# Cluster sums of two units in three from bf16 parts, and the order of work around them

## The chip, the cores and the metric

One core of a Trainium2 chip runs the kernel. The metric is the time of one execution on the device in microseconds, the median over runs. The five engines (TensorE or PE, VectorE or DVE, ScalarE or ACT, GpSimd or POOL, SyncE or SP) each work through a queue of their own in program order and wait for each other by semaphores.

## What is computed

x is 8 batches of 512 channels by 1536 tokens (32 x 48), there are 40 centroids, and W is 512 x 512; all fp32.

```
xn = x / norm(x);  cn = centroids / norm(centroids)
idx = argmax over n of einsum('bchw,nc->bnhw', xn, cn)
onehot = one_hot(idx, N)
sum_x = einsum('bhwn,bchw->bnc', onehot, x)
centroids_local = sum_x / maximum(count, 1.0)
delta = centroids_local[idx] - x
alpha = exp(-mean(delta * delta, over channels))
y = x + alpha * delta
out = relu(einsum('oc,bchw->bohw', W, y) + b)
```

## The kernel before

A batch is cut into PARTS = 3 units of 512 tokens; there are 24 units, g = 3 b + u. For each unit, in the order of the data:

- `similarities` (L728): fp32 matmuls of x with the centroids, in two column tiles of 64 (one for each half of the tokens); `transpose_sims` turns them, and DVE finds the best cluster (`best_sims`, `first_best`, L324 to L339), which gives the one-hots `oh` (fp32). ScalarE makes `oh3` of them, three bf16 copies side by side (`copy_onehot`, L573); `transpose_onehot` (L752) and `evacuate_onehot` (L580) give `ohT`.
- DVE's `transpose_half` (L316) turns x, loaded a second time in blocks of 32 channels (`xs`), into `XT`, token by channel, in two halves a unit. `sum_clusters` (L768) multiplies `oh` and `XT` into the bank `sumP`: per unit two pairs of fp32 matmuls of 512 columns, one of each pair into partitions 0 to 63, the other into 64 to 127. One fp32 matmul of the program is two instructions in the trace.
- `copy_sums`, `low_clusters`, `add_halves`, `scale_means`, `high_means`, `rest_of_mean` and `parts_of_mean` make the means `G` in three bf16 parts.
- `gather` (L799) brings each token its mean (bf16 matmuls), half of the channels at a time; DVE's `delta` (L373) subtracts x; ScalarE's `square` (L531) and DVE's `add_squares`, `fold` and `low_sum` (L391), with ScalarE's `move_upper` and `high_sum` (L540) between, give the sum of squares in a high and a low part; `sum_squares` (L806) adds over partitions, `exp` (L544) makes alpha.
- DVE's `scale` (L397) multiplies by alpha, GpSimd's `y_half` (L286) adds x, ScalarE's `high_half` (L549) rounds y to its high part, GpSimd's `low_half` (L293) takes the low part. In the last units half of these is on DVE (L405, L412).
- `convolve` (L824 to L826): for each of four quarters o of the output channels, 12 matmuls (high x high, low x high, high x low) into one of two banks of `main`; ScalarE's `relu` (L557) empties it. A quarter may start when the quarter two before it is emptied.

The order is written out by hand, for each engine, in a loop over g from 3 to 23. Iteration g gathers unit g, convolves unit g - 2, and scales unit g - 1; p = g mod 3. The work for batch b + 1 stands beside it: with p = 0 and p = 1 (called first and second iteration here) its similarities, with p = 1 its one-hots on DVE, with p = 2 (third iteration) its cluster sums, means and the transposes of the next unit 0. The transposes of unit g + 4 stand in iteration g. GpSimd has a loop of its own over all units: two y halves, two low halves. SP's queue stores, then loads x when y has been made from what it overwrites, then loads `xs`.

The lines that set the places:

```
for g in range(PARTS, UNITS):          # PE
    gather(g, 0)
    if beside and p == 2:
        for u in range(PARTS):
            sum_clusters(b + 1, u)
        gather(g, 1)
        transpose_onehot(b + 1)
        convolve(g - LAG, 0)
        add_halves(b + 1)
```

Of the kernel before, what the change touches and what calls it, by code (L numbers as in the profile page):

```python
# [33 lines left out]

TAIL = UNITS - 1 - PARTS

DIRECT = 2


# [18 lines left out]
    return by_vector, 2 * g + h + 1 - by_vector  # L58


def folded(g):

    return max(0, g + 1 - DIRECT)


def build(nc, x, cent, w, bias, out):
# [3 lines left out]
    with ctx:  # L70
        def sb(name, shape, dt):
            return ctx.enter_context(nc.sbuf_tensor(name, shape, dt))
# [7 lines left out]
        X = [sb(f"x{j}", [P, KC, HW], F32) for j in range(2)]  # L80
        XS = [sb(f"xs{j}", [P, C // BLK, QT], F32) for j in range(2)]
        XT = sb("xt", [P, PARTS, TILES, C], F32)
        Z = [sb(f"z{j}", [P, KC, UNIT], F32) for j in range(2)]
        SQ = sb("sq", [P, 2, UNIT], F32)
        upper_sum = sb("upper_sum", [LOW, UNIT], F32)
# [66 lines left out]
        rc_step, mean_step, rest_step, g_ready = sem("rc_step"), sem("mean_step"), sem("rest_step"), sem("g_ready")  # L152
        gat_done, z_done, sq_done = sem("gat_done"), sem("z_done"), sem("sq_done")
        pair_done, s_done, sh_done, sl_done = sem("pair_done"), sem("s_done"), sem("sh_done"), sem("sl_done")
        upper_done, fold_done = sem("upper_done"), sem("fold_done")
        one_done, exp_done, za_done = sem("one_done"), sem("exp_done"), sem("za_done")
        y_pool, y_dve, hi_done = sem("y_pool"), sem("y_dve"), sem("hi_done")
# [21 lines left out]
        def squares(g, h):  # L179
            if g < DIRECT:  # L180
                return OUT[g][:, pair(h), :]
            return SQ[:, :, :] if h == 0 else gat[:, :, :]

        def plain(b):

# [72 lines left out]
        @block.gpsimd  # L258
        def _(pool):
            pool.memset(ident[:, :], 0.0).then_inc(ident_done, 1)  # L260
            pool.memset(ones[:, :].bitcast(F32), 1.0).then_inc(const_done, 1)
            pool.memset(select0, 0.0).then_inc(ident_done, 1)
            pool.memset(below2[:, :], 0.0).then_inc(ident_done, 1)
            pool.memset(below3[:, :], 0.0).then_inc(ident_done, 1)
            pool.wait_ge(ident_done, 4)
            pool.affine_select(out=ident[:, :], in_=ident[:, :], compare_op=ALU.not_equal, fill=1.0,
                               base=0, pattern=[[-1, P]], channel_multiplier=1).then_inc(ident_done, 1)
            pool.affine_select(out=select_rows, in_=select_rows, compare_op=ALU.not_equal, fill=1.0,
                               base=0, pattern=[[0, COPIES], [-1, N]], channel_multiplier=1).then_inc(ident_done, 1)
            for m, rows in ((below2, N), (below3, 2 * N)):  # L270
                pool.affine_select(out=m[:, :], in_=m[:, :], compare_op=ALU.is_gt, fill=-1.0,
                                   base=rows, pattern=[[0, 1]], channel_multiplier=-1).then_inc(const_done, 1)
            pool.wait_ge(ident_done, 6)
            pool.affine_select(out=select_rows, in_=select_rows, compare_op=ALU.not_equal, fill=1.0,
                               base=-NPAD, pattern=[[0, COPIES], [-1, N]], channel_multiplier=1
                               ).then_inc(ident_done, 1)
            pool.tensor_copy(identb[:, :], ident[:, :]).then_inc(const_done, 1)
            pool.wait_ge(ident_done, 7)
            pool.tensor_copy(select[:, :], select0).then_inc(const_done, 1)

            def y_half(g, h):
                if y_on_vector(g, h):
                    return
                pool.wait_ge(za_done, 2 * g + h + 1)
                z = Z[g % 2][:, pair(h), :]
                pool.tensor_tensor(z, z, X[g // PARTS % 2][:, pair(h), span(g)], ALU.add).then_inc(y_pool, 1)  # L286

            def low_half(g, h):
                if low_on_vector(g, h):
                    return  # L290
                pool.wait_ge(hi_done, 2 * g + h + 1)
                wait(pool, main_done, KC * (g - 1))
                pool.tensor_tensor(YL[g % 2][:, pair(h), :], Z[g % 2][:, pair(h), :],  # L293
                                   YH[g % 2][:, pair(h), :].bitcast(F32), ALU.subtract).then_inc(lo_pool, 1)

            for g in range(UNITS):
                y_half(g, 0)
                y_half(g, 1)
                low_half(g, 0)
                low_half(g, 1)  # L300

        @block.vector
        def _(dve):
# [6 lines left out]
            def transpose_half(g, h):  # L310
                M = C // BLK
                blocks = slice(h * M // 2, (h + 1) * M // 2)
                if h == 0:
                    dve.wait_ge(xs_in[g % 2], 16 * Q * ((g - PARTS) // 2 + 1))
                    dve.wait_ge(c_done, g - PARTS + 1)
                last = v_.transpose(XT[:, g % PARTS, :, :].rearrange("p t (m j) -> p m t j", j=BLK)[:, blocks, :, :],  # L316
                                    XS[g % 2][:, blocks, :])
                if h == 1:
                    last.then_inc(tr_done, 1)

            def best_sims(b):
                dve.wait_ge(simT_done, b + 1)
# [149 lines left out]
            parts_of_mean(1)  # L472
            fold(2)
            low_sum(2)
            transpose_half(6, 0)
            transpose_half(6, 1)
            for g in range(PARTS, UNITS):
                b, p = divmod(g, PARTS)
                beside = b + 1 < BATCH
                delta(g, 0)  # L480
                scale(g - 1, 0)
                scale(g - 1, 1)
                delta(g, 1)
                y_half(g - 1, 1)
                if beside and p < 2:
                    transpose_half(g + 4, 0)
                if beside and p == 2:
                    low_clusters(b + 1)
                    counts(b + 1)
                add_squares(g)  # L490
                if beside and p == 0:
                    transpose_half(g + 4, 1)
                fold(g)
                if beside and p == 2:
                    rest_of_mean(b + 1)
                if beside and p == 1:
                    best_sims(b + 1)
                low_half(g - 1, 1)
                low_sum(g)
                if beside and p == 1:  # L500
                    first_best(b + 1)
                    transpose_half(g + 4, 1)
                if beside and p == 2:
                    parts_of_mean(b + 1)
                    if g + 4 < UNITS:
                        transpose_half(g + 4, 0)
                        transpose_half(g + 4, 1)
            g = UNITS - 1
            scale(g, 0)
            scale(g, 1)  # L510
# [4 lines left out]
        def _(act):  # L515
# [136 lines left out]
            high_means(1)  # L652
            move_upper(2)
            high_half(1, 1)
            high_sum(2)
            relu(0, 2)
            for g in range(PARTS, UNITS):
                b, p = divmod(g, PARTS)
                beside = b + 1 < BATCH
                relu(g - 3, 3)  # L660
                if g > PARTS:
                    exp(g - 1)
                square(g, 0)
                if beside and p == 2:
                    high_half(g - 1, 0)
                    copy_sums(b + 1)
                    evacuate_onehot(b + 1)
                    square(g, 1)
                    high_half(g - 1, 1)
                    relu(g - 2, 0)  # L670
# [5 lines left out]
                else:  # L676
# [9 lines left out]
                    if not beside:  # L686
                        relu(g - 2, 1)
                    move_upper(g)
                    high_half(g - 1, 1)
                    high_sum(g)  # L690
                    if beside:
                        relu(g - 2, 1)
                relu(g - 2, 2)
                if beside and p == 1:
# [14 lines left out]
        def _(pe):  # L709
# [43 lines left out]
                last.then_inc(ohP_done, 1)  # L753

            def sum_clusters(b, u):
                if u == 0:
                    pe.wait_ge(oh_done, b + 1)
                    wait(pe, sumsL_done, b)
                if b > 0:
                    pe.wait_ge(tr_done, PARTS * (b - 1) + u + 1)  # L760
                else:

                    pe.wait_ge(xe_dve, 1)
                    pe.wait_ge(xe_act, 2 * u + 1)
                for t in range(HALF):
                    for h in range(2):
                        tile = HALF * h + t
                        last = t_.matmul(sumP[NPAD * h:NPAD * (h + 1), :], oh[:, slot(u, tile), :],  # L768
                                         XT[:, u, tile, :], start=(u == 0 and t == 0),
                                         stop=(u == PARTS - 1 and t == HALF - 1))  # L770
                last.then_inc(c_done, 1)

            def add_halves(b):
# [148 lines left out]
            for g in range(PARTS, UNITS):  # L922
# [1 line left out]
                beside = b + 1 < BATCH  # L924
                gather(g, 0)
                if beside and p == 2:
                    for u in range(PARTS):
                        sum_clusters(b + 1, u)
                    gather(g, 1)
                    transpose_onehot(b + 1)  # L930
# [41 lines left out]
```

## Time and profile before

| | |
|---|---|
| median of 3 runs | 430.51 us (430.16 to 432.31) |
| profiled execution, its own time | 429.74 us |
| its span, first to last instruction | 427.9 us |
| granted TensorE clock, mean | 1.000 |
| TensorE busy | 416.4 us, 97% |
| TensorE weight loads | 291.1 us, 68% |
| DVE busy | 301.8 us, 71% |
| ScalarE busy | 255.1 us, 60% |
| GpSimd busy | 206.6 us, 48% |
| DMA | 73.94 MB, 173 GB/s |

Busy time is a share of the span. Matmuls are pipelined, so the mean duration of one is longer than the distance to the next; distances between starts tell the rate. In a timeline a row that ends in xN merges N instructions, the second number is the time from the first one's start to the last one's end, and a bracket gives the idle time of that engine just before, with who ended it.

### The profile page before, as it was taken

The numbers are of one execution on the slowest core, as the hardware profiler recorded it, in microseconds if no ns is written. First come the engines' busy times: TensorE is split into PE (matmuls) and PEld (weight loads), VectorE is DVE, ScalarE is ACT, GpSimd is POOL, SyncE is SP. The second block draws the span as 40 slices with busy tenths as digits, with TensorE's granted clock in tenths as the row PEclk, the third lists the DMA queues.
The fourth block names the chain that finished last, engine by engine and source line by source line (L and its number), as shares of the span: only waits on it lengthen the run. The fifth ranks groups of instructions, "written<-read, shape, count | busy, mean of one in ns | idle before, by whom it ended". The sixth has DMA issues, their size and how long they took to land.

```text
span 427.9 us, 5755 instructions
## 1 busy us (share of the span) xinstructions
PE 416.4 (97%) x2106; PEld 291.1 (68%) x2106; DVE 301.8 (71%) x400; ACT 255.1 (60%) x351; POOL 206.6 (48%) x102
## 2 busy tenths in 40 slices
PE   7999998899999999999999999999999999999996
PEld 6744464675867757775767758777677758777785
DVE  2468977687884868678694877958685877788730
ACT  5755383665764675656755666647745657566641
POOL 2000653774563771854744853735816745324320
DMA  8997296867489393966769573983946220222213
GB/s 276 309 285 129 59 266 162 256 192 179 165 207 284 100 243 105 281 159 164 230 164 251 176 185 114 256 232 121 272 90 205 100 98 2 98 100 98 94 68 133
DMA packets 70927, 73.94 MB, mean 173 GB/s; under 512 B 2724, under 2 KB 45732, under 8 KB 70900
## 3 DMA queue, kind: packets, MB, share of 16 engines
q1 hardware_dynamic: 70900, 73.58, 61.6%
q8 instruction: 17, 0.28, 0.3%
q14 instruction: 10, 0.08, 0.1%
HBM read 48.40 MB, written 25.17 MB: 172 GB/s over the span
## 4 chain that ended last, share of the span: by engine, by line
PE 81%; DVE 10%; ACT 3%; issue 2%; DMA 2%; SPq 0%; ACTq 0%; DVEq 0%
PE main L824 17%; PE main L825 16%; PE main L826 16%; PE sump L768 10%; PE fa L728 8%; PE gat L799 5%; DVE z L397 2%; DMA x<-x 2%; DVE z L373 2%; DVE xt L316 1%; PE al L806 1%; PE fa L737 1%; PE fa L752 1%; PE main L867 1%; DVE al L383 1%
## 5 line engine op out<-in xcount | busy, mean ns | idle before, releaser
L286 POOL TENSOR_TENSOR z<-z,x 128x1024 f32<-128x1024 f32 x42 | 99.4, 2386 | 144.8 <-DVE z L397 144.8
L824 PE MATMUL main<-yh,wh 128*128 128x512 f32 x376 | 152.5, 406 | 2.9 <-ACT o L557 2.9
L826 PE MATMUL main<-yh,wl 128*128 128x512 f32 x376 | 146.7, 390 | 0.0
L825 PE MATMUL main<-yl,wh 128*128 128x512 f32 x376 | 146.7, 390 | 0.0
L293 POOL TENSOR_TENSOR yl<-z,yh 128x1024 fp32r<-128x1024 f32 x44 | 105.9, 2423 | 58.6 <-ACT yh L549 58.6
L557 ACT ACTIVATE o<-main,bcol 128x512 f32<-128x512 f32 x96 | 65.1, 682 | 70.9 <-PE main L826 70.9
L373 DVE TENSOR_TENSOR z<-gat,x 128x1024 f32<-128x1024 f32 x46 | 56.2, 1222 | 59.3 <-PE gat L799 59.3
L824 PEld LDWEIGHTS main<-yh,wh 128*128 128x128 f32 x376 | 70.6, 188 | 23.8 <-issue 4.6
L826 PEld LDWEIGHTS main<-yh,wl 128*128 128x128 f32 x376 | 70.6, 188 | 15.2
L825 PEld LDWEIGHTS main<-yl,wh 128*128 128x128 f32 x376 | 70.7, 188 | 13.9
L549 ACT ACTIVATE yh<-z 128x1024 fp32r<-128x1024 f32 x48 | 50.4, 1051 | 22.9 <-POOL z L286 21.9
L397 DVE TENSOR_TENSOR z<-z,al 128x1024 f32<-128x1024 f32 x46 | 54.0, 1213 | 3.5 <-ACT al L544 3.5
L316 DVE STREAM_TRANSPOSE xt<-xs 128x1024 f32<-128x1024 f32 x42 | 51.0, 1230 | 0.0
L728 PE MATMUL fa<-x,c_t 128*64 128x256 f32 x384 | 45.2, 383 | 0.6 <-DMA x<-x 0.3
L768 PE MATMUL sump<-xt,oh 128*64 128x512 f32 x192 | 43.6, 598 | 0.0
L728 PEld LDWEIGHTS fa<-x,c_t 128*64 128x64 f32 x384 | 26.7, 137 | 18.0 <-issue 6.9
L531 ACT ACTIVATE gat<-z 128x1024 f32<-128x1024 f32 x22 | 22.6, 1027 | 20.6 <-DVE z L373 20.6
L531 ACT ACTIVATE sq<-z 128x1024 f32<-128x1024 f32 x22 | 23.3, 1061 | 16.3 <-DVE z L373 16.3
L768 PEld LDWEIGHTS sump<-xt,oh 128*64 128x64 f32 x192 | 12.8, 136 | 25.5 <-issue 25.5
L799 PE MATMUL gat<-oht,g 128*128 128x512 bf16 x92 | 27.8, 384 | 1.1 <-DVE g L366 0.6
L387 DVE TENSOR_TENSOR al<-upper_sum,al 64x512 f32<-64x512 f32 x22 | 15.0, 680 | 10.2 <-ACT upper_sum L535 10.2
L391 DVE TENSOR_TENSOR shl<-al,shl 64x512 fp32r<-64x512 f32 x22 | 15.1, 685 | 6.8 <-ACT shl L540 6.5
(114 smaller groups left out, 335.7 us busy)
## 6 DMA issues: line engine op xcount, KB each, us to landing
x<-x SPq DMA_DIRECT2D x24, 1024.0 KB, 5.7
out<-o SPq DMA_DIRECT2D x23, 1024.0 KB, 5.6
xs<-x SPq DMA_DIRECT2D x84, 256.0 KB, 5.6
o<-w SPq DMA_DIRECT2D x1, 1024.0 KB, 12.2
out<-o SPq DMA_DIRECT2D x4, 256.0 KB, 2.1
sq<-centroids SPq DMA_DIRECT2D x2, 80.0 KB
bcol<-bias SPq DMA_DIRECT2D x1, 2.0 KB, 11.8
```

The source lines that it names most:

```text
L286: pool.tensor_tensor(z, z, X[g // PARTS % 2][:, pair(h), span(g)], ALU.add).then_inc(y_pool, 1)
L293: pool.tensor_tensor(YL[g % 2][:, pair(h), :], Z[g % 2][:, pair(h), :], YH[g % 2][:, pair(h), :].bitcast(F32), ALU.subtract).then_inc(lo_p ...
L316: last = v_.transpose(XT[:, g % PARTS, :, :].rearrange("p t (m j) -> p m t j", j=BLK)[:, blocks, :, :], XS[g % 2][:, blocks, :])
L373: v_.tensor_tensor(Z[g % 2][:, pair(h), :], banks(g, h)[:, :, :], X[g // PARTS % 2][:, pair(h), span(g)], ALU.subtract).then_inc(z_done, 1)
L397: v_.tensor_tensor(z, z, alpha(g).unsqueeze(1).to_broadcast([P, 2, UNIT]), ALU.mult).then_inc(za_done, 1)
L549: a_.activation(YH[g % 2][:, pair(h), :], Z[g % 2][:, pair(h), :], ACT.Copy).then_inc(hi_done, 1)
L557: a_.activation(OUT[g % 2][:, o, :], main[:, o % 2, :], ACT.Relu, bias=bcol[:, o:o + 1]).then_inc(relu_done, 1)
L728: last = t_.matmul(simP[u][NPAD * h:NPAD * (h + 1), :], cT[:, k, :], toks, start=(k == 0), stop=(k == KC - 1))
L768: last = t_.matmul(sumP[NPAD * h:NPAD * (h + 1), :], oh[:, slot(u, tile), :], XT[:, u, tile, :], start=(u == 0 and t == 0), stop=(u == PAR ...
L824: t_.matmul(main[:, o % 2, :], WH[:, k, rows], YH[g % 2][:, k, :], start=(k == 0), stop=False)
L825: t_.matmul(main[:, o % 2, :], WH[:, k, rows], YL[g % 2][:, k, :], start=False, stop=False)
L826: last = t_.matmul(main[:, o % 2, :], WL[:, k, rows], YH[g % 2][:, k, :], start=False, stop=(k == KC - 1))
```

## The change

- In `sum_clusters`, units 0 and 1 of batches 2 to 7 (`split`) are summed from three bf16 parts of x and the bf16 one-hots. The parts are exact: the upper half-word of each fp32 value of `XT`, read in place; the upper half-word of the rest `XR` = x - that, made by GpSimd (`first_rest`); and DVE's remainder (`second_rest`), written into the lower half-word of `XR`. Unit 2, and all units of batches 0 and 1, stay fp32.
- From batch 2 on the third unit's sums come first.
- DVE: `second_rest` at the end of first and second iterations; the transposes of unit 6 move behind the first difference of iteration 3; transposes of units from 9 on wait for the sums of the whole batch before; `low_sum` moves ahead of `low_half`, which matters where DVE has low halves, in the last units.
- ScalarE: in third iterations the copy of the sums and of the one-hots stand ahead of the first high half; in the last batch `high_sum` stands ahead of the second high half; two ReLUs of the prologue stand ahead of `high_sum(2)`.
- GpSimd: `first_rest` behind the low halves of units 1, 2, 4, 5 and so on.
- The scratch for dynamic DMAs is set to 2048.

```diff
+def split(g):
+    return g >= 2 * PARTS and g % PARTS < SPLIT
+def splits(g):
+    return sum(split(i) for i in range(g + 1))
+def sum_order(b):
+    return (2, 0, 1) if b >= 2 else (0, 1, 2)
...
+        XR = sb("xr", [P, SPLIT, TILES, C], F32)
...
+        def halfword(words, which):
+            return words.rearrange("p t c -> p (t c)").bitcast(BF16).rearrange("p (c w) -> p c w", w=2)[:, :, which]
...
+            def first_rest(g):
+                pool.wait_ge(tr_done, g - PARTS + 1)
+                xt = XT[:, g % PARTS, :, :]
+                pool.tensor_tensor(XR[:, g % PARTS, :, :].rearrange("p t c -> p (t c)"),
+                                   xt.rearrange("p t c -> p (t c)"), halfword(xt, 1), ALU.subtract
+                                   ).then_inc(rest1_done, 1)
...
                 low_half(g, 0)
                 low_half(g, 1)
+                if g + 5 < UNITS and split(g + 5):
+                    first_rest(g + 5)
...
-                    dve.wait_ge(c_done, g - PARTS + 1)
+                    dve.wait_ge(c_done, g - PARTS + 1 if g < 3 * PARTS else g // PARTS * PARTS)
...
+            def second_rest(g):
+                dve.wait_ge(rest1_done, splits(g))
+                xr = XR[:, g % PARTS, :, :]
+                v_.tensor_tensor(halfword(xr, 0), xr.rearrange("p t c -> p (t c)"), halfword(xr, 1), ALU.subtract
+                                 ).then_inc(rest2_done, 1)
...
-            transpose_half(6, 0)
-            transpose_half(6, 1)
             for g in range(PARTS, UNITS):
                 b, p = divmod(g, PARTS)
                 beside = b + 1 < BATCH
                 delta(g, 0)
+                if g == PARTS:
+                    transpose_half(g + 3, 0)
+                    transpose_half(g + 3, 1)
...
+                low_sum(g)
                 low_half(g - 1, 1)
-                low_sum(g)
...
+                if g + 3 < UNITS and split(g + 3):
+                    second_rest(g + 3)
...
+            relu(0, 2)
+            relu(0, 3)
             high_sum(2)
-            relu(0, 2)
...
                 if beside and p == 2:
-                    high_half(g - 1, 0)
                     copy_sums(b + 1)
                     evacuate_onehot(b + 1)
+                    high_half(g - 1, 0)
                     square(g, 1)
...
                     move_upper(g)
+                    if not beside:
+                        high_sum(g)
                     high_half(g - 1, 1)
-                    high_sum(g)
                     if beside:
+                        high_sum(g)
                         relu(g - 2, 1)
...
+                x_parts, onehot = (XT[:, u, :, :].rearrange("p t c -> p (t c)"),), oh[:, :, :]
+                if split(PARTS * b + u):
+                    pe.wait_ge(oh3_done, b + 1)
+                    pe.wait_ge(rest2_done, splits(PARTS * b + u))
+                    x_parts = (halfword(XT[:, u, :, :], 1), halfword(XR[:, u, :, :], 1), halfword(XR[:, u, :, :], 0))
+                    onehot = oh3[:, :, 0:NPAD]
                 for t in range(HALF):
-                    for h in range(2):
...
+                    for i, x_part in enumerate(x_parts):
+                        for h in range(2):
+                            tile = HALF * h + t
+                            last = t_.matmul(sumP[NPAD * h:NPAD * (h + 1), :], onehot[:, slot(u, tile), :],
+                                             x_part[:, tile * C:(tile + 1) * C],
+                                             start=(opens and t == 0 and i == 0),
+                                             stop=(closes and t == HALF - 1 and i == len(x_parts) - 1))
...
-                    for u in range(PARTS):
+                    for u in sum_order(b + 1):
                         sum_clusters(b + 1, u)
```

How it stands in the queues. On TensorE, the third iteration g = 5, from its first gather on, before:

```order
L799 MATMUL gat<-oht,g 128x512 x2
L768 MATMUL sump<-xt,oh 64x512 x12
L799 MATMUL gat<-oht,g 128x512 x2
L752 MATMUL fa<-identb,oh 128x4x32 x12
```

and after (`xt` is x transposed, `xr` the rests, `oh` here both `oh` and `oh3`):

```order
L855 MATMUL gat<-oht,g 128x512 x2
L823 MATMUL sump<-xt,oh 64x512 x6
L823 MATMUL sump<-xr,oh 64x512 x4
L823 MATMUL sump<-xt,oh 64x512 x2
L823 MATMUL sump<-xr,oh 64x512 x4
...
L823 MATMUL sump<-xr,oh 64x512 x4
L855 MATMUL gat<-oht,g 128x512 x2
```

12 fp32 matmuls became 4 fp32 ones (in the first row, with the first two bf16 ones of unit 0) and 24 bf16 ones. On GpSimd, from the y halves of unit 2 on, before:

```order
L286 TENSOR_TENSOR z<-z,x 128x1024 x2
L293 TENSOR_TENSOR yl<-z,yh 128x1024 x2
L286 TENSOR_TENSOR z<-z,x 128x1024 x2
L293 TENSOR_TENSOR yl<-z,yh 128x1024 x2
L286 TENSOR_TENSOR z<-z,x 128x1024 x2
```

and after:

```order
L324 TENSOR_TENSOR xr<-xt 128x2048
L310 TENSOR_TENSOR z<-z,x 128x1024 x2
L317 TENSOR_TENSOR yl<-z,yh 128x1024 x2
L324 TENSOR_TENSOR xr<-xt 128x2048
L310 TENSOR_TENSOR z<-z,x 128x1024 x2
L317 TENSOR_TENSOR yl<-z,yh 128x1024 x2
L310 TENSOR_TENSOR z<-z,x 128x1024 x2
L317 TENSOR_TENSOR yl<-z,yh 128x1024 x2
```

A `first_rest` stands ahead of the y halves of two units in three. On DVE, the end of the second iteration g = 4 and the start of the third, after (before there is no `xr` row):

```order
L431 TENSOR_TENSOR shl<-al,shl 64x512
L369 TENSOR_TENSOR fa<-fa,best 128x12x40
L372 TENSOR_TENSOR rank<-fa,weight 128x480
L375 TENSOR_REDUCE fa<-rank 128x12
L379 TENSOR_TENSOR oh<-rank,fa 128x12x40
L350 STREAM_TRANSPOSE xt<-xs 128x8x4x32
L358 TENSOR_TENSOR xr<-xr 128x2048
L413 TENSOR_TENSOR z<-gat,x 128x1024
```

The `second_rest` stands between the last transpose and the next difference.

## Rows read from the trace of the kernel before

**Rows 1.** The page: TensorE's busy time; the chain's shares of the span.

```profile
PE 416.4 (97%) x2106; PEld 291.1 (68%) x2106; DVE 301.8 (71%) x400; ACT 255.1 (60%) x351; POOL 206.6 (48%) x102
...
PE 81%; DVE 10%; ACT 3%; issue 2%; DMA 2%; SPq 0%; ACTq 0%; DVEq 0%
```

**Rows 2.** The chain that ended last: start us, us, what.

```profile
149.83 5.30 PE sump L768 x24
...
198.73 0.45 PE gat L799 x2
199.18 5.30 PE sump L768 x24
...
236.89 1.88 PE fa L728 x16
```

**Rows 3.** Busy time by stretch: a batch; the last batch.

```profile
core 0: us, PE busy (x) PEld busy (x) DVE busy (x) ACT busy (x) POOL busy (x), PEclk, DMA share, GB/s
...
199.00:248.00 49.00, 49.00 (x251) 34.64 (x251) 36.66 (x44) 30.10 (x43) 28.37 (x12) 1.00 0.70 193
...
365.00:403.00 38.00, 37.38 (x163) 28.63 (x162) 31.22 (x33) 25.55 (x35) 14.41 (x6) 1.00 0.22 83
```

**Rows 4.** Timeline of TensorE, second and third iteration.

```profile
186.94 0.61 PE L799 MATMUL gat<-oht,g 128*128 128x512 bf16 x2
...
195.61 0.39 PE L824 MATMUL main<-yh,wh 128*128 128x512 f32 x1
...
199.10 5.37 PE L768 MATMUL sump<-xt,oh 128*64 128x512 f32 x24
```

**Rows 5.** Timeline of GpSimd, one batch.

```profile
186.82 4.74 POOL L286 TENSOR_TENSOR z<-z,x 128x1024 f32<-128x1024 f32 x2 [6.42 <-DVE z L397]
191.51 4.75 POOL L293 TENSOR_TENSOR yl<-z,yh 128x1024 fp32r<-128x1024 f32 x2
201.64 4.70 POOL L286 TENSOR_TENSOR z<-z,x 128x1024 f32<-128x1024 f32 x2 [5.38 <-DVE z L397]
...
220.30 4.72 POOL L286 TENSOR_TENSOR z<-z,x 128x1024 f32<-128x1024 f32 x2 [8.66 <-DVE z L397]
```

**Rows 6.** Timeline of DVE, second iteration to the next second one.

```profile
194.35 0.68 DVE L391 TENSOR_TENSOR shl<-al,shl 64x512 fp32r<-64x512 f32 x1 [0.32 <-ACT shl L540]
...
197.60 1.24 DVE L316 STREAM_TRANSPOSE xt<-xs 128x1024 f32<-128x1024 f32 x1
...
200.35 2.34 DVE L397 TENSOR_TENSOR z<-z,al 128x1024 f32<-128x1024 f32 x2
205.05 1.23 DVE L373 TENSOR_TENSOR z<-gat,x 128x1024 f32<-128x1024 f32 x1 [2.35 <-PE gat L799]
...
214.46 2.36 DVE L316 STREAM_TRANSPOSE xt<-xs 128x1024 f32<-128x1024 f32 x2
...
233.73 1.23 DVE L373 TENSOR_TENSOR z<-gat,x 128x1024 f32<-128x1024 f32 x1 [5.06 <-PE gat L799]
```

**Rows 7.** Timeline of ScalarE, second and third iteration.

```profile
192.65 1.05 ACT L549 ACTIVATE yh<-z 128x1024 fp32r<-128x1024 f32 x1
...
194.22 0.67 ACT L557 ACTIVATE o<-main,bcol 128x512 f32<-128x512 f32 x1
...
204.05 1.06 ACT L549 ACTIVATE yh<-z 128x1024 fp32r<-128x1024 f32 x1 [2.52 <-POOL z L286]
```

**Rows 8.** Groups: the similarity matmuls (busy us, mean ns, idle before).

```profile
L728 PE MATMUL fa<-x,c_t 128*64 128x256 f32 x384 | 45.2, 383 | 0.6 <-DMA x<-x 0.3
```

**Rows 9.** Timelines of DVE and GpSimd where they meet.

```profile
46.10 1.23 DVE L405 TENSOR_TENSOR z<-z,x 128x1024 f32<-128x1024 f32 x1
...
46.42 5.52 POOL L293 TENSOR_TENSOR yl<-z,yh 128x1024 fp32r<-128x1024 f32 x2 [43.35 <-ACT yh L549]
...
404.87 2.40 POOL L286 TENSOR_TENSOR z<-z,x 128x1024 f32<-128x1024 f32 x1 [4.82 <-DVE z L397]
...
405.95 2.39 DVE L405 TENSOR_TENSOR z<-z,x 128x1024 f32<-128x1024 f32 x1
```

**Rows 10.** TensorE's waits near both ends; GpSimd's y pair of unit 2.

```profile
66.58 0.50 PE L824 MATMUL main<-yh,wh 128*128 128x512 f32 x1 [1.18 <-ACT o L557]
...
73.68 4.77 POOL L286 TENSOR_TENSOR z<-z,x 128x1024 f32<-128x1024 f32 x2 [7.11 <-DVE z L397]
...
81.96 0.50 PE L824 MATMUL main<-yh,wh 128*128 128x512 f32 x1 [1.76 <-ACT o L557]
...
377.45 0.47 PE L806 MATMUL al<-shl,ones 128*128 128x512 f32 x1 [0.22 <-DVE shl L391]
```

**Rows 11.** DMA issues: size and median us to landing.

```profile
x<-x SPq DMA_DIRECT2D x24, 1024.0 KB, 5.7
```

More of the change, by code:

```diff
@@ L35 @@
 TAIL = UNITS - 1 - PARTS
+SPLIT = 2
 DIRECT = 2
@@ L154, in build @@
         pair_done, s_done, sh_done, sl_done = sem("pair_done"), sem("s_done"), sem("sh_done"), sem("sl_done")
+        rest1_done, rest2_done = sem("rest1_done"), sem("rest2_done")
         upper_done, fold_done = sem("upper_done"), sem("fold_done")
@@ L659, in _ @@
                 beside = b + 1 < BATCH
-                relu(g - 3, 3)
                 if g > PARTS:
+                    relu(g - 3, 3)
                     exp(g - 1)
@@ L755, in sum_clusters @@
             def sum_clusters(b, u):
-                if u == 0:
+                opens, closes = u == sum_order(b)[0], u == sum_order(b)[-1]
+                if opens:
                     pe.wait_ge(oh_done, b + 1)
@@ L764, in sum_clusters @@
                     pe.wait_ge(xe_act, 2 * u + 1)
-                for t in range(HALF):
-                    for h in range(2):
[L767 to L770, printed above, removed]
+                x_parts, onehot = (XT[:, u, :, :].rearrange("p t c -> p (t c)"),), oh[:, :, :]
[4 more added lines that the diff above has]
+                    onehot = oh3[:, :, 0:NPAD]
+                for t in range(HALF):
+                    for i, x_part in enumerate(x_parts):
[5 more added lines that the diff above has]
+                                             stop=(closes and t == HALF - 1 and i == len(x_parts) - 1))
                 last.then_inc(c_done, 1)
@@ L956 @@
     from concourse.bass_utils import run_bass_kernel_spmd
-    nc = bacc.Bacc("TRN2", target_bir_lowering=False, num_devices=1)
+    nc = bacc.Bacc("TRN2", target_bir_lowering=False, num_devices=1, dynamic_dma_scratch_size=2048)
     x = np.asarray(x)
```

## The prediction

> **What bounds the kernel now.** I read the page first. TensorE is busy 97% of the span and holds 81% of the chain that ended last [rows 1], so time comes off only where TensorE's work or its few waits do. The merged chain shows the steady state: the 24 instructions of a batch's cluster sums take 5.30 us and come back every 199.18 - 149.83 = 49.35 us, one batch [rows 2]. In that stretch TensorE has no idle time, DVE is busy 37 of 49 us, ScalarE 30, GpSimd 28 [rows 3]. So a microsecond less of TensorE work is a microsecond less per batch, as long as nobody becomes later than TensorE. The order rows above show what is new in each queue; the timelines of TensorE and of the three others [rows 4 to 7] say how late each may be. All clock times below are those of the batch whose sums start at 199.10 [rows 4]; times of before from its next batch on are those rows plus 49.35.
>
> **Part 1, the sums on TensorE.** Today a pair of column tiles (tokens h=0 and h=1) of fp32 matmuls costs 5.30 / 6 = 0.88 us. In units 0 and 1 of batches 2 to 7 it becomes three bf16 pairs. No row shows a bf16 pair of 64 columns. Its nearest rows: the similarity matmuls, where two column-tile instructions that each stream 2 x 256 columns share 45.2 / 192 = 0.235 us [rows 8]; and the bf16 gather, 0.45 us for two full-width matmuls, 0.225 each [rows 2]. If the tiles overlap as in fp32, a bf16 pair costs 0.225 to 0.235; I take 0.23, so 0.69 per three. Saved: 0.19 x 4 pairs = 0.76 us per batch, **4.6 us in six batches**. The bad bound is that the tiles don't overlap: 3 x 0.45 = 1.35, a loss of 0.47 x 24 = 11 us. I take the good end, since both column-tiled groups (fp32) overlap. Unit 2 stays fp32 and goes first, so the bf16 one-hots (ready 199.1, as the sums start) have 1.77 us of cover.
>
> **Part 2, the two rests.** Six times each for unit 0 and unit 1: GpSimd makes x minus its high half (2048 columns), DVE then splits that. GpSimd's pairs of 1024 columns follow each other by 4.69 us (186.82 to 191.51) [rows 5]; one instruction in place of two spares a start, so I take 4.6 (ends 4.4 and 4.7; half-words with a stride have no row). [...] DVE: two of 1024 columns take 2.34 (at 200.35 [rows 6]), so 2.2 us (ends 2.2 and 4.4).
> DVE's rest reads two SBUF tensors, and such instructions exclude GpSimd: at 405.95 DVE's add took 2.39 us in place of 1.2, having to wait until GpSimd's instruction (404.87 for 2.40) ended, and at 46.42 GpSimd's pair took 5.52 instead of 4.7 behind a DVE add from 46.10 [rows 9]. In the steady state of before no DVE instruction is of this kind; now two per batch are, and they count on both engines.
>
> **Part 3, follow GpSimd through a batch.** Its queue gets a rest behind the low halves of the third and the first iteration.
> - DVE's two transposes of the third iteration end at 216.8 [rows 6]. The change puts one of ScalarE's high halves (1.0 each, [rows 7]) ahead of the square there, and the shorter sums give back 0.76: 217.05. The first rest runs 217.15 to 221.75. The y pair behind it, at 220.30 today [rows 5], runs to 226.45, the low pair to 231.15.
> - DVE, which idled 5.06 us before 233.73 [rows 6], asks for its rest at 228.9 (the second high half at 226.5, the low sum 1.70 later, 0.7 long), while GpSimd is in its second low half. I let it in when that ends, 231.15 to 233.35.
> - For the next difference that is 0.4 late, which has slack.
> - The rest of unit 1 runs to 237.95, the y pair of the second iteration to 242.65.
> - ScalarE's second high half waits for that pair. Today it starts at 192.65 and the ReLU of output quarter 1, two places behind it, ends at 194.89, 2.24 later [rows 7]: now 242.7 and 244.95.
> - TensorE needs this ReLU before quarter 3: at 195.61 today [rows 4], now 195.61 + 49.35 - 0.76 = 244.2. **It stalls 0.8 us.**
> - DVE's low sum waits for ScalarE too: it starts 1.70 after that high half (194.35), and one-hots and the last transpose end 4.49 later (198.84) [rows 6]: now 244.4 and 248.9. TensorE now opens with unit 2, whose transpose is that last one; it would start the sums at 199.10 + 49.35 - 0.76 + 0.8 = 248.5 and gets them at 248.95. **It stalls 0.45 us more.**
> - DVE's second rest (GpSimd is idle then, 196.3 to 201.6 today [rows 5]) delays the next difference by 2 us. DVE has 2.35 us idle ahead of 205.05 [rows 6], and ScalarE 2.52 at 204.05 that the moved copy of the sums now uses [rows 7], so this I cost at nothing.
> Per batch: -0.76 + 0.8 + 0.45 = +0.5 us; six batches, **+2.9 us**.
>
> **Part 4, the edges.** In the last batch ScalarE and DVE now take the sum of squares ahead of the high and low half. TensorE waits 0.22 us for it, three times over, and is idle 0.62 of 38 us [rows 3, 10]: **-0.6**. In the prologue the ReLU ahead of the high sum and the delayed transposes of unit 6 free TensorE's 1.18 us at 66.58; but the next stall, 1.76 us at 81.96 [rows 10], hangs on the y pair of 73.68 [rows 10], and now a rest stands in front of it (about 70.2 to 74.8): it starts 1.1 later, and the relief is given back. 0. The scratch size and the coarser wait of the transposes (sums already over) cost nothing; SP's loads wait for y and the transposes, some 3 us later at worst, but the tightest x slice has 11.9 us from its y (220.30 + 4.72 [rows 5]) to the similarities (236.89 [rows 2]) and lands in 5.7 [rows 11]; were that cover gone, TensorE would wait for x there.
>
> **Sum:** +2.9 - 0.6 = +2.3 on the profiled execution's 429.74, 432.0. That execution lies 0.77 under the median 430.51, to which I set the forecast: **432.8 us**. By itself it lies in 429.5 to 435.5, since each clock in Part 3 may be off by half a microsecond six times.
>
> **Rivals.**
> - *GpSimd is not the bound.* The chain of Part 3 has only to be 1.25 us shorter per batch (rests of 4.0 us instead of 4.6, or a DVE rest that overlaps) and both stalls vanish; then all of Part 1 remains: -4.6 - 0.6 = 425.3, less up to 1 in the prologue. For it: GpSimd's share only grows from 28 to 38 of 49 us. Against: it is a chain of waits, not a share, and no row has so short a rest. 0.34.
> - *DVE starves.* No row shows who gets the turn when GpSimd's instructions follow back to back. If GpSimd does, DVE's rest waits from 228.9 to the end of GpSimd's second rest, 235.75, and ends at 237.95; the difference that the iteration's second gather needs ends at 239.15, while TensorE is there at 186.94 [rows 4] + 49.35 - 0.76 = 235.5. A stall of 3.7 in place of 0.8 and 0.45 is +2.9 per batch: 447. Decided by whether DVE waits past one GpSimd instruction. 0.10.
> - *Half-words are slow*, on any of three engines. [...] No row here has such operands. 0.09.
> - *The sums do not shrink*, tiles not overlapping or half so: TensorE's own time grows up to 11 us, 437 to 443. 0.05.
>
> **How the numbers follow.** A measurement tells this kernel from no change at about 0.5%, 2.2 us: same is 428.4 to 432.7. The forecast case has 0.42, of which 0.22 slower, 0.17 same, 0.03 faster; the first rival 0.34, of which 0.32 faster and 0.02 same; the other three 0.24, slower. In all 0.35 faster, 0.19 same, 0.46 slower. The forecast and the first rival lie apart, so the range reaches over both, 425 to 438.5; it leaves out the starvation and the worse halves of the slow cases.
>
> **What would show it.** Right: sums of some 4.5 us in place of 5.3; GpSimd 38 us busy per batch; TensorE waits of about 0.8 us on ScalarE's ReLU at quarter 3 of second iterations and 0.4 at the start of the sums; a period of 49.85. Wrong: a period of 48.6 without a TensorE wait (first rival); DVE rests of 8 us (starvation); rests of 3.7 without waiting; bf16 pairs well over 0.24.

## The result and the profile after

| | before | after |
|---|---|---|
| median | 430.34 us (429.74 to 432.31) | 424.90 us (424.58 to 425.02) |
| runs | 6 | 6 |
| span of the profiled execution | 427.9 us | 422.8 us |

The change makes the kernel faster: ratio 0.9869, 95% interval 0.9849 to 0.9889. The forecast was 432.8 us, slower, and the range of 425 to 438.5 just misses the time; the first rival, "GpSimd is not the bound", gave 425.3.

This is the chain that ended last, after (start us, us, what), to be read against [rows 2]:

```profile
149.53 4.58 PE sump L823 x32
...
197.71 0.45 PE gat L855 x2
198.16 4.58 PE sump L823 x32
```

A batch now takes 198.16 - 149.53 = 48.63 us in place of 49.35, and all of the 0.72 is in the sums, 4.58 for 5.30. TensorE waits for nobody in the steady state, which the stretches show too (columns as in [rows 3]):

```profile
199.00:248.00 49.00, 49.00 (x263) 35.04 (x261) 44.25 (x47) 30.87 (x43) 37.85 (x14) 1.00 0.71 194
...
365.00:403.00 38.00, 38.00 (x168) 30.21 (x167) 32.52 (x34) 24.62 (x34) 16.23 (x7) 1.00 0.24 90
```

DVE is up from 37 to 44 us of 49, GpSimd from 28 to 38 (the time in which one of them waits for the other counts as busy). So the new work is there and hidden. GpSimd's and DVE's timelines show how (answering to [rows 5] and [rows 6]):

```profile
178.20 2.41 POOL L317 TENSOR_TENSOR yl<-z,yh 128x1024 fp32r<-128x1024 f32 x1
180.56 5.99 POOL L324 TENSOR_TENSOR xr<-xt 128x2048 f32<-128x2048 f32 x1
186.51 4.76 POOL L310 TENSOR_TENSOR z<-z,x 128x1024 f32<-128x1024 f32 x2
...
216.21 3.60 POOL L324 TENSOR_TENSOR xr<-xt 128x2048 f32<-128x2048 f32 x1 [4.10 <-DVE xt L350]
219.76 4.73 POOL L310 TENSOR_TENSOR z<-z,x 128x1024 f32<-128x1024 f32 x2
224.46 4.75 POOL L317 TENSOR_TENSOR yl<-z,yh 128x1024 fp32r<-128x1024 f32 x2
```

```profile
178.36 4.76 DVE L358 TENSOR_TENSOR xr<-xr 128x2048 bf16<-128x2048 f32 x1
183.37 1.22 DVE L413 TENSOR_TENSOR z<-gat,x 128x1024 f32<-128x1024 f32 x1 [0.24 <-PE gat L855]
...
197.74 2.57 DVE L358 TENSOR_TENSOR xr<-xr 128x2048 bf16<-128x2048 f32 x1
```

GpSimd's rest takes **3.60 us** where nothing disturbs it (216.21), not the 4.6 of the forecast. The other one (180.56) takes 5.99: DVE asked for its rest at 178.36, GpSimd's low half ended at 180.56, and DVE's rest ran to 183.12 ahead of GpSimd's. So GpSimd's 5.99 are 2.4 of waiting and 3.6 of work.

Hidden doesn't mean that there is much room. At the two places where the forecast saw a stall, ScalarE's ReLU now ends 0.71 us ahead of quarter 3, and DVE's last transpose (196.58 + 1.24 = 197.82) ends 0.26 us ahead of the sums (rows of the three timelines, after):

```profile
193.20 0.68 ACT L600 ACTIVATE o<-main,bcol 128x512 f32<-128x512 f32 x1
194.59 0.39 PE L880 MATMUL main<-yh,wh 128*128 128x512 f32 x1
...
196.58 1.24 DVE L350 STREAM_TRANSPOSE xt<-xs 128x1024 f32<-128x1024 f32 x1
...
198.08 2.16 PE L823 MATMUL sump<-xt,oh 128*64 128x512 f32 x10
```

The 5.1 us of span come from three places. Six batches of sums give 6 x 0.72 = 4.3. The last batch gives 1.2: from its first gather to the last ReLU it ran from 365.42 to 424.74 before and runs from 361.52 to 419.60 after. The prologue *loses*: batch 2's sums start at 100.90 and not 100.48, 0.4 later. This is TensorE's timeline there, after (against [rows 10]), and two stretches of it (columns as in [rows 3]):

```profile
80.77 0.50 PE L880 MATMUL main<-yh,wh 128*128 128x512 f32 x1 [2.58 <-ACT o L600]
...
82.68 0.63 PE L880 MATMUL main<-yh,wh 128*128 128x512 f32 x1
83.10 0.63 PE L881 MATMUL main<-yl,wh 128*128 128x512 f32 x1
83.53 0.63 PE L882 MATMUL main<-yh,wl 128*128 128x512 f32 x1
```

```profile
75.00:80.00 5.00, 3.19 (x15) 2.30 (x13) 3.35 (x5) 3.53 (x5) 5.00 (x3) 1.00 0.87 262
80.00:85.00 5.00, 4.23 (x12) 3.37 (x13) 4.79 (x2) 1.29 (x3) 5.00 (x3) 0.68 1.01 287
```

The wait of 1.76 us has become 2.58, though TensorE comes to it earlier and goes on earlier too, at 80.77 and not 81.96. Behind it, from 81.8 to 84.8, the matmuls follow each other by 0.43 us in place of 0.23; the granted clock is 0.68 over the stretch from 80 to 85 us, and 0.50 from 82 to 85. Before, behind 1.76 us, the distance stayed 0.23 and the granted clock 1.00 (80 to 85 us).

From there to the next gather TensorE takes 4.68 us (80.77 to 85.45) where it took 3.09 before (81.96 to 85.05), which turns a lead of 1.2 us into the loss of 0.4. Yet the low clock isn't shown to be the cause of the loss. Of the four executions of `full_word` below, whose instructions take the same times, two had a mean granted clock of 1.000 and took 424.70 and 424.56 us, two had 0.996 and took 424.69 and 424.68. A second chain lies close behind: GpSimd's second rest of this batch waits for DVE's,

```profile
83.04 5.94 POOL L324 TENSOR_TENSOR xr<-xt 128x2048 f32<-128x2048 f32 x1
```

and through the y pair behind it, ScalarE and DVE, the last transpose ends at 100.55, 0.28 us ahead of the sums (100.83 in the timeline). If that chain stays where it is, no more than this 0.28 can come back with the clock. No kept trace shows an execution of this kernel without the drop.

### The profile page after: what moved, and what is told of

Its sections match the earlier page's. It is cut to its first block, busy times and chain, and to the rows that moved or that the text cites. A ratio compares the mean times of both kernels' runs of the same rounds, so it can differ in the third digit from the quotient of the medians.

```text
span 422.8 us, 5887 instructions
## 1 busy us (share of the span) xinstructions
PE 412.9 (98%) x2154; PEld 293.7 (69%) x2154; DVE 344.3 (81%) x412; ACT 256.4 (61%) x351; POOL 263.5 (62%) x114
## 4 chain that ended last, share of the span: by engine, by line
PE 90%; POOL 2%; DVE 2%; ACT 2%; DMA 1%; issue 1%; SPq 0%
PE main L880 20%; PE main L881 19%; PE main L882 19%; PE sump L823 9%; PE fa L774 9%; PE gat L855 5%; DMA x<-x 1%; PE fa L783 1%; PE al L862 1%; POOL z L310 1%; PE fa L798 1%; PE main L923 1%; DVE xt L350 1%; PE al L868 1%; PE gat L868 1%
## 5 line engine op out<-in xcount | busy, mean ns | idle before, releaser
L324 POOL TENSOR_TENSOR xr<-xt 128x2048 f32<-128x2048 f32 x12 | 57.4, 4786 | 24.2 <-DVE xt L350 24.2
L358 DVE TENSOR_TENSOR xr<-xr 128x2048 bf16<-128x2048 f32 x12 | 43.9, 3658 | 0.2
L823 PE MATMUL sump<-xt,oh 128*64 128x512 f32 (+1 forms) x144 | 31.5, 532 | 0.0
```

Source lines behind the costliest of these rows:

```text
L324: pool.tensor_tensor(XR[:, g % PARTS, :, :].rearrange("p t c -> p (t c)"), xt.rearrange("p t c -> p (t c)"), halfword(xt, 1), ALU.subtract ...
L823: last = t_.matmul(sumP[NPAD * h:NPAD * (h + 1), :], onehot[:, slot(u, tile), :], x_part[:, tile * C:(tile + 1) * C], start=(opens and t = ...
```

## The experiments

Each is the changed kernel with one edit; times stand against the changed kernel's 424.9.

**1. Is it the half-word operand that makes GpSimd's rest cheap?** `full_word`:

```diff
-   xt.rearrange("p t c -> p (t c)"), halfword(xt, 1), ALU.subtract
+   xt.rearrange("p t c -> p (t c)"), xt.rearrange("p t c -> p (t c)"), ALU.subtract
```

> The changed kernel, but GpSimd's rest subtracts the fp32 x from itself in place of its upper half-words (so the rest is zero and the cluster sums lose their lower parts). Theory A (the step that failed was the price of GpSimd's rest: 3.60 us with a bf16 half-word operand, where I took 4.6 from fp32 rows; with two fp32 operands the rest costs 4.5 to 4.7 and the chain through GpSimd binds): rests without contention take 4.5 to 4.7 us, TensorE waits about 1 us on ScalarE's ReLU in second iterations, the period is 49.5 to 50.2 us in place of 48.63, the time 430 to 434 us. Theory B (the chain had more slack than I reckoned whatever the rest costs): the period stays 48.6 to 48.8 and the time under 427.

424.68 us, and the rests take 3.60 as before. The time is theory B's, but neither theory is shown: two full fp32 operands cost no more, so the cheapness is not in the half-words, the rest did not become dearer, and the chain was not put to the test.

**2. Size, or which tensors?** `rest_halves` (two instructions of 1024 columns), `rest_other` (in1 is W's high part) and later `rest_swap` (each half subtracts the other half):

```diff
+   for s in (slice(0, 1024), slice(1024, 2048)):
+       last = pool.tensor_tensor(XR[...][:, s], xt[...][:, s], halfword(xt, 1)[:, s], ALU.subtract)
```

```diff
-   xt.rearrange("p t c -> p (t c)"), halfword(xt, 1), ALU.subtract
+   xt.rearrange("p t c -> p (t c)"), WH[:, :, :].rearrange("p k c -> p (k c)").bitcast(F32), ALU.subtract
```

```diff
+   for s, o in ((slice(0, 1024), slice(1024, 2048)), (slice(1024, 2048), slice(0, 1024))):
+       last = pool.tensor_tensor(XR[...][:, s], flat[:, s], flat[:, o], ALU.subtract)
```

> The changed kernel with GpSimd's rest as two instructions of 1024 columns. GpSimd's other pairs of 1024 columns take 4.7 us, its rest of 2048 takes 3.60 with half-words and with full words alike. Theory S (a fixed cost of about 1.1 us per GpSimd instruction, so that size makes the difference): the two halves take 4.6 to 4.8 us. Theory O (what differs is which memory the operands come from: the rest reads one tensor twice): they take 3.6 to 3.8. If they take 4.7, this is also the kernel that my forecast priced, and the chain through GpSimd should stall TensorE about 0.8 us per batch: 430 us; with full slack 425.

> The changed kernel with GpSimd's rest subtracting W's high part (another SBUF tensor of 2048 fp32 columns) in place of x's own half-words, so the cluster sums are wrong in their lower parts. Theory O (reading one tensor twice is what is cheap): the rest takes 4.5 to 4.8 us. Theory S (size): it stays at 3.60.

> The changed kernel with GpSimd's rest in two instructions of 1024 columns, each subtracting the other 1024 columns of the same fp32 tensor (the sums are wrong in their lower parts). Two halves with both operands at the same place took 3.75 us, one instruction with operands from two tensors 4.60. Theory P (what is cheap is that both operands lie at the same addresses): the pair takes 4.7 us and the time goes to 434 to 436. Theory T (it is enough that both lie in one tensor): 3.75 us and 424.9.

GpSimd's timeline, first rest of a batch and what follows it, `rest_halves`:

```profile
216.35 3.75 POOL L325 TENSOR_TENSOR xr<-xt 128x1024 f32<-128x1024 f32 x2 [4.11 <-DVE xt L352]
220.05 4.74 POOL L310 TENSOR_TENSOR z<-z,x 128x1024 f32<-128x1024 f32 x2
```

`rest_other`:

```profile
221.56 4.60 POOL L325 TENSOR_TENSOR xr<-xt,wh 128x2048 f32<-128x2048 f32 x1 [4.12 <-DVE xt L351]
226.12 4.74 POOL L310 TENSOR_TENSOR z<-z,x 128x1024 f32<-128x1024 f32 x2
```

`rest_swap`, the pair of halves:

```profile
234.80 4.73 POOL L326 TENSOR_TENSOR xr<-xt 128x1024 f32<-128x1024 f32 x2 [4.79 <-DVE xt L352]
239.49 4.72 POOL L310 TENSOR_TENSOR z<-z,x 128x1024 f32<-128x1024 f32 x2
```

Size costs 0.15 us, not 1.1. With operands at the same addresses a 2048-column subtraction takes 3.60 (one fp32, one half-word, or both fp32), with operands at different addresses 4.60 (two tensors) or 4.73 in two halves (one tensor, 1024 columns apart). Theories O and P hold, S and T fall. (The granted clock of TensorE was 0.853 in the profiled execution of `rest_swap`; GpSimd's y pair takes 4.72 in it as elsewhere.) Why equal addresses are cheaper no run here says, and no other distance between the operands was tried.

The times of the three are 424.91, **434.54** and 436.73 us. The middle one has the rest that the forecast priced.

**3. Does a dearer rest bind, and where?** `rest_plus` repeats the first 512 columns behind each rest:

```diff
+   pool.wait_ge(rest0_done, splits(g))
+   pool.tensor_tensor(XR[...][:, 0:512], xt[...][:, 0:512], halfword(xt, 1)[:, 0:512], ALU.subtract)
```

> The changed kernel with a second GpSimd instruction behind each rest that repeats its first 512 columns (same values): the rest becomes 3.6 us plus some 0.9 to 1.5. Theory A (the forecast's chain through GpSimd was right and only the rest was priced 1.0 too dear; the room left is about 0.5 per rest): TensorE waits on ScalarE's ReLU in second iterations by 0.5 to 1.5 us, the period is 49.3 to 50.2 us, the time 429 to 434. Theory B (there is room the chain did not count): the period stays 48.63, the time under 426.

435.99 us, ratio to before 1.0144 (1.0129 to 1.0159): 1.04 us on each of 12 GpSimd instructions makes 11.1 us. That is theory A, and by more than its 429 to 434: the sums stand 50.56 us apart, so 1.93 of the 2.08 us added per batch come through, and the room is nearer to the 0.26 us above than to the 0.5 per rest that was expected. TensorE's timeline of `rest_other`, two batches, shows the two waits that the forecast named:

```profile
199.25 0.50 PE L881 MATMUL main<-yh,wh 128*128 128x512 f32 x1 [0.95 <-ACT o L601]
203.29 2.16 PE L824 MATMUL sump<-xt,oh 128*64 128x512 f32 x10 [0.35 <-DVE xt L351]
...
249.56 0.50 PE L881 MATMUL main<-yh,wh 128*128 128x512 f32 x1 [0.96 <-ACT o L601]
253.60 2.16 PE L824 MATMUL sump<-xt,oh 128*64 128x512 f32 x10 [0.30 <-DVE xt L351]
```

and its chain (start us, us, what), where GpSimd leads from the rest to the y pair, then ScalarE, DVE and the last transpose:

```profile
235.57 5.92 POOL xr L325
241.49 0.95 issue
242.45 4.79 POOL z L310 x2
...
248.35 0.60 ACT shl L584
...
248.97 0.68 DVE shl L432
...
252.22 1.24 DVE xt L351
```

The period is 253.60 - 203.29 = 50.31 us, 1.68 over that of the changed kernel. The two brackets hold 1.3 of it; they count from the modelled end of the matmul before, so the period is the better measure.

**4. A guess at a faster GpSimd**: `low_flat` gives the low halves as one row of 1024 in place of 2 x 512.

> The changed kernel with GpSimd's low halves given as one row of 1024 columns in place of 2 x 512 (the rest is given flat too, the low and y halves are not). Theory F (the form 2 x 512 is what makes them dear): a low half takes 1.8 us in place of 2.35. Otherwise it stays 2.35 and the time 424.9.

424.70 us; a low half still takes 2.4. The form is not it. The guess missed, and the miss agrees with experiment 2: the operands of a low half are two tensors.

**5. What do the rests cost?** `no_rests`:

```diff
-   if g + 5 < UNITS and split(g + 5):
-       first_rest(g + 5)
...
-   if g + 3 < UNITS and split(g + 3):
-       second_rest(g + 3)
...
-   x_parts = (halfword(XT[:, u, :, :], 1), halfword(XR[:, u, :, :], 1), halfword(XR[:, u, :, :], 0))
+   x_parts = (halfword(XT[:, u, :, :], 1),) * 3
```

> The changed kernel without the two rests: all three bf16 passes read the upper half-words of x (the sums are then three times the upper part, not x), GpSimd and DVE lose 12 instructions each. If the rests cost nothing in the steady state, the period stays 48.63 us. If the rest of unit 6 on GpSimd is what holds TensorE 2.58 us at 80.77 and drops its clock, that wait shrinks and the clock stays up: 1.5 to 2.5 us less in all, 422.4 to 423.4. If the rests cost something in each batch as well, it is under 422.

422.11 us. In the steady state the rests cost nothing: the chain's sum rows stand 48.63 us apart without them (195.54, 244.16, 292.79). All of the 2.8 us is won in the prologue, where batch 2's sums start at 98.28 and not 100.90; the wait is 1.38 us and the mean granted clock of the run 1.000 for 0.996. This kernel takes away the rests of GpSimd and of DVE, the long wait and the drop of the clock at once, so it doesn't say which of them costs the 2.8.

**6. Take the cost out of the prologue.** `late_split` splits from batch 3 on, `mid_split` from unit 7 on, `y_first` moves one instruction:

```diff
-    return g >= 2 * PARTS and g % PARTS < SPLIT
+    return g >= 3 * PARTS and g % PARTS < SPLIT
```

```diff
-    return g >= 2 * PARTS and g % PARTS < SPLIT
+    return g > 2 * PARTS and g % PARTS < SPLIT
```

```diff
                 y_half(g, 1)
+                if g == 2:
+                    first_rest(6)
                 low_half(g, 0)
```

> The changed kernel with the split from batch 3 on, not 2: no rest of units 6 and 7, batch 2's sums in fp32 (third unit first). It gives back 0.72 us of sums and takes GpSimd's rest from in front of the y halves of unit 2. Theory A (that rest and the clock drop behind the wait cost 2 us): 424.9 + 0.7 - 2.0 = 423.6. Theory B (the wait at 80.77 is there for another reason, as before had 1.76 us at 81.96): 425.6.

> The changed kernel with the split from unit 7 on: unit 6 stays fp32, so GpSimd has no rest in front of the y halves of unit 2, but units 7 and on are summed in bf16. Against the split from batch 3 on (422.9) unit 7 saves another 0.36 us if its rests cost nothing: 422.5. If its rest, at about 83 us, still delays the y halves of unit 3 past their slack, 423.5 or more.

> The changed kernel with one instruction moved: GpSimd's rest of unit 6 behind the y halves of unit 2 in place of ahead of them. The y halves then start at about 71.3 and not 73.7, ScalarE's second high half of unit 2 about 2.3 us earlier. Theory A: the wait of 2.58 us at 80.77 falls to about 0.5, the clock stays at 1.0 from 80 to 85 us, and the time is 422.5 to 423.2. Theory B (low halves and DVE's rest of unit 6, now 3.6 us later, hold TensorE instead): 424.5 to 425.5.

`late_split`: 422.89 us, theory A, and 0.7 below its 423.6. TensorE's wait:

```profile
79.69 0.50 PE L880 MATMUL main<-yh,wh 128*128 128x512 f32 x1 [1.36 <-ACT o L600]
```

with a granted clock of 1.00 from 80 to 85. `mid_split`: **422.34 us**, close to the 422.5 of a rest of unit 7 that costs nothing (the wait is 1.37), ratio to before 0.9818 (0.9793 to 0.9843), the fastest that computes all of the reference; its interval overlaps that of `late_split` (0.9822 to 0.9851), so only the gain over the changed kernel is clear. With unit 7's rests in place it is within 0.3 us of `no_rests`, so nearly all of the 2.8 hangs on the rests of unit 6. `y_first`: 425.53, theory B. The first wait falls to 1.33 and the mean granted clock is 1.000, but DVE's rest takes its turn in front of the low halves, and TensorE waits for those:

```profile
80.06 7.09 POOL L317 TENSOR_TENSOR yl<-z,yh 128x1024 fp32r<-128x1024 f32 x2
```

```profile
87.30 0.47 PE L882 MATMUL main<-yh,wh 128*128 128x512 f32 x1 [2.14 <-POOL yl L317]
```

**7. Are the two moves needed?** `act_order` (the first high half ahead of the copies again) and `unit_order` (units 0, 1, 2):

```diff
+                    high_half(g - 1, 0)
                     copy_sums(b + 1)
                     evacuate_onehot(b + 1)
-                    high_half(g - 1, 0)
```

```diff
-    return (2, 0, 1) if b >= 2 else (0, 1, 2)
+    return (0, 1, 2)
```

> The changed kernel with ScalarE's old order in third iterations: the first high half ahead of the copies of sums and one-hots. The high half waits for GpSimd's first y half, which ends at 205.0 in the changed kernel, where the copy of the sums now starts at 202.8. Theory A (this move is needed because DVE's rest delays the y halves): the copies end some 2.5 us later, TensorE waits for them ahead of the addition of the halves by 1 to 2 us per batch, 430 to 436 us. Theory B (the copies have slack): 424.9.

> The changed kernel with the sums of units 0, 1, 2 in this order in every batch. Unit 1's bf16 sums would start at about 199.5 and its DVE rest ends at 200.3. Theory A: TensorE waits 0.8 us per batch at unit 1, period 49.4, time 429 to 430. Theory B (the order doesn't matter): 424.9.

Both are. `act_order`: 434.11 us; ScalarE's high half waits for GpSimd, and TensorE for the copy behind it, in each batch. The first row is ScalarE's, the others are TensorE's in two earlier batches:

```profile
208.30 1.06 ACT L592 ACTIVATE yh<-z 128x1024 fp32r<-128x1024 f32 x1 [2.54 <-POOL z L310]
```

```profile
110.94 0.50 PE L835 MATMUL fa<-sums_h,select 128*128 128x512 f32 x1 [1.33 <-ACT oht L623]
161.13 0.50 PE L835 MATMUL fa<-sums_h,select 128*128 128x512 f32 x1 [1.32 <-ACT oht L623]
```

Before, in the same order, the high half waited as long, 2.52 us [rows 7], and TensorE for nobody behind it. But there the wait ended 4.95 us after the sums began (204.05 against 199.10), and here 6.95 (208.30 against 201.35), since DVE's rest stands in front of what the y half needs, and the sums are 0.72 shorter.

`unit_order`: 431.03 us, 1 us above theory A's 430, the whole gain gone (ratio to before 1.0016, 0.9988 to 1.0043); the sums wait twice:

```profile
100.99 0.42 PE L823 MATMUL sump<-xt,oh 128*64 128x512 bf16 x2 [0.18 <-ACT oh L616]
103.09 0.42 PE L823 MATMUL sump<-xt,oh 128*64 128x512 bf16 x2 [0.55 <-DVE xr L358]
```

## Why the prediction was wrong

**The step that failed is the price of GpSimd's rest in Part 2.** I took 4.6 us, with ends 4.4 and 4.7, from GpSimd's pairs of 1024 columns; it took 3.60, outside both. The rows were right for what they show: instructions whose operands come from two tensors. With such operands the rest does take 4.60 (experiment 2), and that kernel takes 434.54 us where the forecast said 432.8. The bound had no row for "x minus its own upper half", and I set its ends from the same rows.

Point by point:

- *What bounds the kernel*: right. A us of TensorE work was a us of time; the period fell by just what the sums lost.
- *Part 1*: right. The two tiles of a bf16 pair overlap: (4.58 - 1.77) / 12 = 0.234 us a pair for the 0.23 taken, where one full-width matmul of the gather takes 0.225; 0.72 per batch for 0.76. The fp32 tiles overlap in the trace of before too: its full-width fp32 matmuls of 512 columns follow each other by 0.43 us (L812, eight from 37.73 to 41.16), those of the sums by 5.30 / 24 = 0.22.
- *Part 2, exclusion and turn*: right. DVE's first rest of a batch waited for GpSimd's running instruction and then went ahead of the next, in every one of the six (DVE's took 4.67 to 4.76 us, GpSimd's behind it 5.94 to 5.99); the rival of starvation was not seen. DVE's rest alone takes 2.57, not 2.2.
- *Part 3*: the chain is real, its stalls were not there. It has 2 us less in it (two rests, each 1.0 cheaper), and I had it 1.25 beyond its slack. With the dear rest both stalls appear at the places named, 0.96 (forecast 0.8) and 0.30 to 0.35 (0.45); the period is 50.31 (49.85). So place and sign of the mechanism were right and one term was mis-sized, by the amount that decided. The rest of the chain was a little too short: by its sum 0.75 us of room would be left with the cheap rests, and 0.26 is.
- *The costs set at nothing*: the rest before the third iteration is hidden as said, but only with ScalarE's move (without it 434.1), and the bf16 one-hots and DVE's rest only behind the third unit's sums (431.0). The forecast was right to count on these covers but did not price their absence.
- *Part 4*: the last batch gave 1.2 for 0.6; I had counted the idle time (0.62), and the period of its iterations went from 12.50 to 12.05 us, three times. That ScalarE's and DVE's new order there did it is read from waits that are gone, and no run takes those moves back alone; nor the ones of the prologue. In the prologue I said nothing won, nothing lost; it lost 0.4, and without the rests it would have won 2.2 (batch 2's sums at 98.28 in `no_rests`, 100.48 before).
- *The range*: its lower end stood just under the first rival's 425.3, and left out most of that rival's "up to 1 in the prologue". The rival's sum was right: 429.74 - 5.2 = 424.54 for the profiled execution, which took 424.58. In part that is luck, since the sums gave 0.3 less, the last batch 0.6 more and the prologue lost 0.4. The miss came from the 0.77 us by which before's median of three lay over its profiled execution and which I added; after the change the median lies only 0.32 over. The first rival had 0.34, the forecast case 0.42: too sure of a sum in which the 1.25 us per batch beyond the slack hung on one unmeasured price taken twice.
- *Half-words are slow*: refuted on all three engines. TensorE 0.234 a pair; GpSimd 3.60 with and without; DVE 2.57 where it ran alone, 0.2 over the 2.34 of two of 1024 columns (for DVE no run has the same instruction with full words). No row or run shows the 3.7 us of DVE's rest by which this rival was to be known.

## What to carry to other kernels

When a forecast hangs on a new instruction sitting in a loop of waits, price it from both sides by rows of the same kind of operands, and if there are none, widen the bound until it reaches the point where the loop stops binding; the loop's slack (0.26 us per batch here), not the instruction's cost, is then the number to give. Work moved onto two engines of a bound kernel is free only behind named covers: here each of two moves that look cosmetic carried the whole gain. In a prologue the first use of a new helper instruction can be left out for the price of one unit, and that was the better kernel.

## What the runs showed of the hardware

- GpSimd's subtraction of 2048 columns took 3.60 us when both operands were read at the same addresses (fp32 with fp32, `full_word`, or with the upper half-words of the same words, the changed kernel), and 4.60 when they came from two tensors (`rest_other`). In two halves it took 3.75 at the same addresses (`rest_halves`) and 4.73 from one tensor 1024 columns apart (`rest_swap`).
- The times of DVE's rest, whose two operands lie in SBUF, and of GpSimd's instructions add up as if the two ran one after the other. Where both queued, DVE got the turn at the end of GpSimd's running instruction, six times of six: DVE's 4.76 us at 178.36 are 2.2 of waiting and 2.56 of work (2.57 where it ran alone, at 197.74), and GpSimd's next took 5.99 (3.60 where nothing disturbed it, at 216.21).
- TensorE's granted clock fell behind a wait of 2.58 us (0.68 from 80 to 85 us) and did not behind one of 1.76 (before) or 1.36 (`late_split`).
